# A two-layer hypergraph network: eight PSUM banks in one ring, batches written out, edge weights loaded early, and another opening

## The reference

```
H  = (adj != 0);  w = adj[first row]
Dn = 1 / (H @ w);  Be = 1 / H.sum(axis=1)
conv(x, W, b) = Dn * (H @ (Be * (H^T @ (x @ W^T)))) + b
h0 = relu(layernorm(x))
h  = layernorm(relu(conv(h0, W1, b1))) * gamma + beta
out = x + h0 + conv(h, W2, b2)
```

## Time and profile before

| | |
|---|---|
| three runs | 691.07, 691.65, 693.44 us |
| median | 691.65 us |
| profiled execution, span from first to last instruction | 692.0 us |
| TensorE busy | 636.5 us (92%), 4744 matmuls |
| VectorE busy | 510.2 us (74%) |
| ScalarE busy | 294.0 us (42%) |
| GpSimd busy | 83.6 us (12%) |
| mean granted clock of TensorE | 0.973 of full |

### The profile page before, as it was taken

How to read it: one execution, slowest core, us unless ns; L and a number is a source line. 1 busy time by engine, 2 the same in 40 slices (tenths; PEclk the granted TensorE clock), 3 DMA queues, 4 the chain that set the end, 5 groups by cost and what they waited for, 6 DMA issues and landing times.

```text
span 692.0 us, 12544 instructions
## 1 busy us (share of the span) xinstructions
PE 636.5 (92%) x4744; PEld 468.2 (68%) x4744; DVE 510.2 (74%) x1224; ACT 294.0 (42%) x538; POOL 83.6 (12%) x48
## 2 busy tenths in 40 slices
PE   4675999999989989999998998999999899999997
PEld 3432575778756776668756686586885578676886
DVE  6999877996479954799467984689747996558732
ACT  4144384354252642535415362254624364223720
POOL 2426002001120020200202002020022002000000
PEclk9888899999998999999999999999999999999999
DMA  8984960009940099302990059800796009500701
GB/s 318 230 326 92 333 123 1 1 1 197 262 182 1 1 222 291 129 1 31 235 346 29 1 103 201 337 1 1 151 238 251 1 1 229 107 1 0 183 2 62
DMA packets 146221, 90.38 MB, mean 131 GB/s; under 512 B 134768, under 2 KB 135408, under 8 KB 141168
## 3 DMA queue, kind: packets, MB, share of 16 engines
q1 hardware_dynamic: 146160, 89.54, 49.5%
HBM read 47.58 MB, written 8.39 MB: 81 GB/s over the span
## 4 chain that ended last, share of the span: by engine, by line
DVE 33%; PE 32%; SPq 11%; DMA 8%; issue 7%; ACT 7%; DVEq 0%; ACTq 0%
PE narrow L463 9%; SPq L241 8%; PE narrow L475 7%; PE wide L432 7%; DVE incidence L719 6%; DVE junk L728 5%; PE wide L416 4%; DMA edge_weights<-adj 4%; DMA z<-z_split_ring 3%; PE narrow L451 3%; DVE stat L704 3%; DVE z L785 2%; SPq L248 2%; DVE stat L789 2%; DVE h_split L710 2%
## 5 line engine op out<-in xcount | busy, mean ns | idle before, releaser
L463 PE MATMUL narrow<-xw_split,incidence 128*128 128x256 f16 x1024 | 118.4, 279 | 9.5 <-DVE edge_means L824 9.5
L463 PEld LDWEIGHTS narrow<-xw_split,incidence 128*128 128x128 bf16 x1024 | 101.9, 100 | 26.1 <-DVE edge_means L824 10.8
L416 PE MATMUL wide<-incidence_t,edge_means 128*128 128x512 bf16 x512 | 115.1, 386 | 3.9 <-DVE edge_means L862 3.9
L475 PE MATMUL narrow<-edge_means,incidence_t 128*128 128x256 f16 x1024 | 114.1, 273 | 1.5 <-DVE residual L843 1.5
L475 PEld LDWEIGHTS narrow<-edge_means,incidence_t 128*128 128x128 bf16 x1024 | 99.7, 98 | 16.1 <-DVE residual L843 3.1
L397 PE MATMUL narrow<-h_split,incidence 128*128 128x257 f16 x448 | 99.0, 273 | 4.7 <-DVE edge_means L862 4.6
L511 ACT ACTIVATE edge_means<-narrow,edge_inverse 128x256 f16<-128x256 f32 x124 | 57.4, 475 | 105.0 <-PE narrow L463 64.7
L728 DVE SCALAR_TENSOR_TENSOR junk<-incidence,edge_weights 128x1024 f32<-128x1024 bf16 x64 | 77.7, 1215 | 28.9 <-DMA edge_weights<-adj 28.9
L399 PE MATMUL narrow<-h_split,incidence 128*128 128x256 f16 x448 | 98.9, 273 | 0.0
L416 PEld LDWEIGHTS wide<-incidence_t,edge_means 128*128 128x128 f16 x512 | 50.6, 99 | 65.4 <-DVE edge_means L862 5.3
L451 PE MATMUL narrow<-w_split,z 128*128 128x256 f16 x768 | 87.7, 276 | 7.7 <-issue 6.7
(11 more groups left out here) (89 smaller groups left out, 640.2 us busy)
## 6 DMA issues: line engine op xcount, KB each, us to landing
adj_in<-adj SPq DMA_DIRECT2D x32, 1024.0 KB, 11.7
out<-residual SPq DMA_DIRECT2D x32, 256.0 KB, 2.8
x_in<-x SPq DMA_DIRECT2D x7, 1024.0 KB, 6.6
edge_weights<-adj SPq DMA_DIRECT2D x8, 512.0 KB, 4.9
x_in<-x SPq DMA_DIRECT2D x2, 512.0 KB, 4.6
z<-w2t SPq DMA_DIRECT2D x1, 512.0 KB, 5.6
z<-w1t SPq DMA_DIRECT2D x1, 512.0 KB, 8.3
incidence_t<-incidence SPq DMA_TRANSPOSE x32, 5.4
```

The lines of the kernel that those rows point to most:

```text
L416: last = nc.tensor.matmul(wide[j][:, :], edge[:, et, part, P * dt:P * (dt + 1)], inc_t[:, b.slot, 4 * half:4 * (half + 1), et, :], start=( ...
L463: last = nc.tensor.matmul(acc[:, 0:DOUT], inc[:, b.slot, ct, P * et:P * (et + 1)], xw[:, ct, part, :], start=(ct == 0 and part == HI), sto ...
L475: last = nc.tensor.matmul(acc[:, 0:DOUT], inc_t[:, b.slot, ct, et, :], edge[:, et, part, :], start=(et == 0 and part == HI), stop=(et == T ...
```

## The change

- PSUM becomes one tensor `acc` of eight banks, and `place` gives each tile of each stage its bank, in the order in which the stages run. Each stage waits for the drain of the tile that had the bank eight tiles before. Counts of edges are read four at a time.
- The loops of all engines are written out.
- `step` loads the edge weights first, before the stores, not behind the transposes of H.
- GpSimd adds h0 and b2 in eight pieces each instead of four and one; in batches 0 and 1 it adds b2 first and h0 after.
- Opening: b2 and adj come right after x; W1 is loaded behind two transposes of H, beta, gamma and W2 later still. The x statistics of batch 0 are made in two halves. Degrees 0 to 3 come before the edge means, 4 to 7 behind. The factor of W1 is found and applied alone before B's drains of batch 0; W2 is multiplied with beta and gamma, its largest found and W2 scaled only when z of batch 0 has its statistics. Incidence and h0 of batch 1 are made between the drains of C of batch 0, the z statistics behind them. x and adj of batch 2 are loaded behind the turned z of batch 0.

```diff
+        acc_ring = ctx.enter_context(nc.psum_tensor("acc", [P, RING, BANK], F32))
+            if stage == "A":
+                at = (0, 3 * T)[k] if opening else 8 * T + 4 + PER_BATCH * (k - 2)
+            elif stage == "B":
+                at = T if first else 5 * T + PER_BATCH * (k - 1)
+            elif stage == "C":
+                at = T + 4 if first else 6 * T + 4 + PER_BATCH * (k - 1)
+            elif stage == "D":
+                at = 4 * T + PER_BATCH * k - (T if last else 0)
+            elif stage == "E":
+                at = 5 * T + 4 + PER_BATCH * k - (T + 4 if last else 0)
+            else:
+                at = 7 * T + 4 + PER_BATCH * k - (2 * T + 4 if last else 0)
+            return (at + i) % RING
...
             def step(b, load=True, turn_h=True, turn_z=True):
+                if turn_h:
+                    load_edge_weights(b.next(2))
                 for q in range(QUARTERS):
...
                     for q in range(QUARTERS):
                         transpose_inc(b.next(2), q)
-                    load_edge_weights(b.next(2))
...
+                for t in range(T):
+                    pool.wait_ge(u_ready, b.count(T, t + 1))
+                    nc.gpsimd.tensor_tensor(x_in[:, t, :], x_in[:, t, :], u[:, t // GT % 2, t % GT, :],
+                                            ALU.add).then_inc(x_added, 1)
...
             def stage_a(b):
-                        acc = take_narrow(b, et, t1_ready, out_ready, b.next(-2))
+                    pe.wait_ge(out_ready, b.next(-2).count(T, et + 1))
...
             def stage_b(b):
-                        pe.wait_ge(c_drained, b.count(T, 5 + j - T))
+                        pe.wait_ge(xf_ready, b.next(-1).count(T, j + 1))
...
             def stage_c(b):
-                    if t >= 4:
-                        pe.wait_ge(c_drained, b.count(T, t - 3))
+                    if not (isinstance(b.loop, int) and b.offset == 0):
+                        pe.wait_ge(t2_ready, b.next(-1).count(T, t + 1))
...
             def stage_d(b):
-                        acc = take_narrow(b, t, xf_ready, t1_ready, b.next(1))
+                        pe.wait_ge(t1_ready, b.next(1).count(T, t + 1))
...
             def stage_e(b):
-                    acc = take_narrow(b, et, t2_ready, xf_ready, b)
+                    elif et < 4:
+                        pe.wait_ge(xf_ready, b.count(T, et + 5))
+                    else:
+                        pe.wait_ge(pt_ready, b.next(1).count(4, et - 3))
...
             def stage_f(b):
-                    acc = take_narrow(b, ct, out_ready, t2_ready, b)
+                        pe.wait_ge(c_drained, b.next(1).count(T, ct + 1))
...
-            with pe.Fori(0, N - 2, 2) as n:
-                for k in range(2):
...
+            for n in range(N - 2):
+                stage_d(Batch(0, n))
+                stage_b(Batch(0, n + 1))
```

ScalarE's opening:

```diff
+            act.wait_ge(w1_scale, 5)
             copy(w1s[:, :, HI, :], w1f, scale=wr[:, 2:3])
             copy(w1f, w1f, scale=wr[:, 2:3]).then_inc(w_hi, 1)
+            drain_b(b0, 0)
...
+            z_split(b0, 0)
+            z_split(b0, 1)
+            act.wait_ge(w2_scale, 5)
             copy(w2s[:, :, HI, :], gf, scale=wr[:, 3:4])
             copy(gf, gf, scale=wr[:, 3:4]).then_inc(w_hi, 1)
             for t in range(T):
+                if t >= 2:
+                    z_split(b0, t)
+                t1_hi_part(b1_, t)
```

VectorE's opening:

```diff
+            for ct in range(4):
+                degree(b0, ct)
+            for half in range(2):
+                edge_inverse(b0, half)
+                for et in range(T // 2 * half, T // 2 * (half + 1)):
+                    t1_lo_part(b0, et)
+            dve.wait_ge(w1_loaded, 16)
+            largest(0, w1f).then_inc(max_here, 1)
+            degree(b0, 4)
+            degree(b0, 5)
+            factor(0, w1_scale, 1.0 / (H0_SCALE * PT_SCALE * W_SCALE))
+            b_lo(b0, 0)
+            b_lo(b0, 1)
+            degree(b0, 6)
+            degree(b0, 7)
...
+            inverse_root(z_ln, z_step, b0, Z_STEPS, ZN_SCALE)
             dve.wait_ge(gamma_w2, 1)
+            largest(1, gf).then_inc(bias_step, 1)
...
+            z_lo(b0, 0)
+            z_lo(b0, 1)
+            factor(1, w2_scale, 1.0 / (ZN_SCALE * W_SCALE * XW_SCALE))
```

493 lines of the change are left out of this document (300 added, 193 removed).

## The result

| | before | after |
|---|---|---|
| median, us | 692.55 (691.07 to 693.69, 4 runs) | 662.48 (661.79 to 663.38, 4 runs) |
| ratio | | 0.9555, 95% interval 0.9528 to 0.9582 |
| span of the profiled execution, us | 692.0 | 661.6 |
| opening: stage B of batch 1 starts at | 106.55 | 107.50 |
| from there to the end of the span | 585.45 | 554.10 |

The forecast was 666.0 us, so the sign, the size and in the main the mechanism were right, and 3.5 us were left over. The table already says where the gain is: all of it behind 107.50, and the rebuilt opening is 0.95 us longer than the old one.

A forecast was written before the change was run, and what follows sets the result against it. TensorE was taken to bound the kernel behind 106.55 us, VectorE in the opening. Opening 111.2 + rest 554.6 + 0.5 for small waits gave 666.3 us of span, 0.35 over the median: 666.0 us, range 655 to 678.

The forecast's parts named there:

- Parts 1 to 3: Behind the opening: early edge weights, eight banks and written-out loops together return 30.4 of 30.9 us lost.
- the ring: Eight PSUM banks in one ring: drain waits of stages A and F and slow matmuls behind them go, 6 to 8 us.
- the jumps: TensorE's two jumps back in its loop: writing it out removes both gaps and the slow D, 8.4 us.
- Part 4: Rebuilt opening: z may be split from 83.7, but stage B of batch 1 starts at 111.2, 4.7 us later than before.
- the second all-reduce: Opening, GpSimd's maximum for W2: largest at 85.0, all-reduce ends at 89.7, dependent factor steps at 90.8.
- only its shown 0.37, 106.9: Bound for the opening: if the W2 all-reduce costs only its shown 0.37 us, B of batch 1 starts at 106.9.
- GpSimd's lock: Opening: GpSimd's adds stop VectorE; smaller pieces lose 14 us instead of 18, a gain of 4.
- The first: Rival: opening gains too, GpSimd's pieces fall between VectorE's, B of batch 1 starts near 100, total 655 us; chance 0.18.
- The second: Rival: written-out code stalls at the same places from code fetch, the 8.4 us stay, 674 us; chance 0.08.
- the fourth: Rival: TensorE waits a little at many tiles, 678 us, or 757 with some stages at 1.2 GHz; chance 0.05.
- The third: Rival: opening loses to GpSimd tiles between 13 dependent statistics steps or slow D pairs, 673 to 675 us; chance 0.15.
- The fifth: Rival: GpSimd's sixteen pieces a batch delay VectorE, bound beyond 0.7 us a piece, 723 us at 1.2; chance 0.04.

The follow-up runs named there:

- both2: Changed kernel with b2 additions moved later, W2 scaled before the z split, and bias, node factor and first edge inverse ahead of two low z parts: 654.59 us.
- pool_whole: Changed kernel with GpSimd's adds from batch 2 on in the old large pieces, four and one of 2048 columns: 661.97 us.
- early: Kernel before with only the edge weights loaded early, at the head of SyncE's step: 675.00 us.
- both: Changed kernel with the b2 additions moved to stage E of batch 0 and W2 scaled before the z split: 656.77 us.
- w2_early: Changed kernel with W2, gamma and beta loaded earlier and W2 scaled before the z split: 662.36 us.
- base_whole: Changed kernel with GpSimd's first b2 addition in batches 0 and 1 as one operation of 2048 columns: 667.01 us.

## Why the prediction was right, and where it was off

The sum had 111.2 us of opening and 555.1 behind it, 666.3 of span. Measured were 107.50 and 554.10: 3.7 and 1.0 less. Between span and median lay 0.9 us instead of the -0.35 I took. That makes 3.5.

The -0.35 had the wrong sign. The profiled execution of after took 663.38 us, 1.8 more than its own span, and in the twelve other kernels the difference is 1.7 to 2.1. The 692.0 of before was the span of one execution, set beside the median of others. With 1.8 the forecast would have been 668; that the printed one is nearer is luck.

**Parts 1 to 3 in sum: right.** Of the 30.9 us lost behind the opening I gave back 30.4; 31.35 came back. Reading the plain length of each stage off the trace of before and adding them up gave the floor to half a microsecond, 554.6 against 554.10, and eight kernels reached it within 0.3. The 0.5 us for small new waits wasn't needed. A slip inside the 30.9: 0.5 of A's 4.6 us of waits lies ahead of 106.55, so F and D had 1.8 and not 1.3.

**The shares of the parts: right in the total, too simple one by one.** They aren't terms of a sum. With the old banks the early weights are worth 18.8 us in the loop and 25.1 (583.32 to 558.26) with it written out; in the ring 13.1. Writing out is worth 2.1, 8.35 or 7.3. The ring, with the smaller edits that no run separates from it, is worth 4.2 when the other two are there, and 16.1 (583.32 to 567.23) when the weights are late. My 8.4 for the jumps was right only in company; my 6 to 8 for the ring was too high, since F's waits and a part of A's went with the late weights. Also the new load isn't issued "early in stage E" but at E's end, behind the last degree:

```profile
134.15 0.33 SPq L272 DMA_DIRECT2D edge_weights<-adj  x1
```

E runs to 135.28 there. A load lands 3.7 us later (median), and the one of the next batch, issued at 211.64, is first used at 256.38: the cover is 40 us, far more than the 14 I named.

**Part 4: direction right, 3.7 us too dear.** Step by step from the same points:

| | forecast | measured |
|---|---|---|
| z split starts | 83.7 | 82.25 |
| second factor ready | 90.8 | 86.6 |
| W2's two copies done | 92.9 | 88.8 |
| z split done on ScalarE | 104.4 | 100.7 |
| B of batch 1 starts | 111.2 | 107.50 |

The mis-sized term is the second all-reduce. In the kernel before it stood 4.7 us between input and result, and I took that as its own cost. VectorE and ScalarE of after:

```profile
83.48 0.16 DVE L1086 SCALAR_TENSOR_TENSOR weight_max<-weight_max 128x1 f32<-128x1 f32 x1
...
85.21 0.69 DVE L913 TENSOR_TENSOR z_split_ring<-z,z_split_ring 128x512 f16<-128x512 f32 x1 [0.70 <-ACT z L632]
85.82 0.15 DVE L1001 TENSOR_SCALAR weight_max_all<-weight_max_all 128x1 f32<-128x1 f32 x1
...
82.25 0.81 ACT L631 ACTIVATE z_split_ring<-z,z_ln 128x512 f16<-128x512 f32 x1
...
86.62 1.15 ACT L592 ACTIVATE w_split<-xw_split,weight_factor 128x1024 f16<-128x1024 f32 x1 [1.45 <-DVE weight_factor L1009]
```

The input is complete at 83.64, the result is there at 84.16: 0.5 us, and the factor then waits only for VectorE's own low part of z, to 85.82. The 4.7 us was a delay that runs from the end of GpSimd's operation before; there that was 28.04, 1.2 us ahead of the input, and here GpSimd had been idle for 13.08 us. The page of before had said so: "5.59 <-issue" in the earlier trace rows is idle time with nothing to wait for, and I read past the word. I had the other end of the bound, "only its shown 0.37, 106.9", 0.6 us from what was measured, which is in part luck (below); the value was taken from the nearest row, which stood under another condition.

Not all of the 3.7 us is this term. 1.45 of it is there before, with the z split's start. The all-reduce was 4.2 us too dear, but since the factor then waited for VectorE, the stretch from z split to factor is only 2.75 shorter than forecast (4.35 instead of 7.1); the six tiles behind it took some 0.5 longer. So 106.9 came close by errors that cancelled. And the sign "GpSimd's second all-reduce in the chain that ended last" didn't come: the chain runs through VectorE's second low part to the factor.

The same mechanism on the other side I missed: an ordinary operation behind an all-reduce starts 7 to 9 us late. It costs C 2.5 and D 4.1 us of waiting; D's first tiles start at 93.71 where its z was turned sooner. It is worth 1.4 us at most, since A and C of the opening have room.

**Smaller terms.** GpSimd's lock: the sixteen incidence rows of the opening take 14.2 us instead of 24.1, the eight low parts 6.9 instead of 7.8, and single steps lose some 7.5 (4.4 in those of 128x4; of those of 128x8 the largest is 2.10 us instead of 0.17, at 48.76, beside the subtraction for W1); about 13 lost where I took 14. The term was right, and gives 1 of the 1.45 us by which the z split came early; A of batch 0 took 3.3 us more than its plain length (17.33 instead of 14.03, last section). "As many microseconds in total" was wrong: the tiles take 0.85 us each in the steady part and not 0.6. A of batch 0 ended at 34.44 (forecast 31), C at 61.26 (58), A of batch 1 began at 73.30 (74), and the hole before it was there, from the end of C to 73.30.

**The rivals.** The first (opening near 100) didn't come about, but its room was real: both2 takes it, at 99.36. The second (gaps in straight code) and the fourth (small waits at many tiles) are excluded by 0.11 us of idle time in 550.96. With the fourth falls the reading that goes with it: by the Trainium skill ("TensorE: Matmul & The Clock Gate", A second HAM failure mode: psum-queue depth-cycling) a kernel that cycles through banks can swing between both clock levels; here the clock stayed at 1.00 through some 300 tiles of such cycling, so the trace gives no instance of it. The third had its mechanism right, dependent steps each behind a tile, and its price too high: five steps of 0.65 and a few others, not thirteen for each set. The fifth was nearer than its 0.04 allowed by my own rule: a piece takes 0.85 us and the rule had VectorE the bound from 0.7 on. Yet nothing was lost, and pool_whole shows the pieces cost nothing: the rule charged each piece in full to VectorE, whose busy time behind the opening instead is 401.81 us with the small pieces in after and 407.22 with the large ones in pool_whole.

## What to carry to other kernels

Add up the undisturbed lengths of the bound engine's stages from the trace of before: that floor forecast this result better than any account of the single waits, because such waits share causes and an edit that removes one alone may only move it (2.1 us alone, 8.35 with the other). More buffers take in late drains, not late data: first find the load that the engine in the middle waits for. And where a row gives the cost of an operation, look whether its idle time says "issue" before taking the distance from input to result as the operation's own.

## What was not expected of the hardware

GpSimd loses time when it changes between an all-reduce and an ordinary addition, unless the time is hidden by a longer wait for the input. The all-reduce starts 5.5 to 6.4 us after the end of the ordinary operation before it though its input is there (5.59, 5.53 in early, 6.11 and 5.99 in the rows above, 6.35 in both), and 0.1 to 0.3 us after its input when GpSimd has been idle for 13 us or more. The way back takes 8.67 and 7.20 us in after, 7.42 and 6.73 in w2_early and both2 for W2, and 6.7 to 8.7 in every kernel with the new opening and an all-reduce, but for W1 in both and both2: there it takes 10.77 and 11.70, and C waits 4.6 and 5.5 us for it. What makes these two longer is open. By the Trainium skill ("GPSIMD Engine Reference", Instruction dispatch) the first call of a freshly loaded routine pays about 6 us that no instruction in the profile shows. The trace agrees in size for the way there, with 5.5 to 6.4; it also shows it again at the second all-reduce and, longer, on the way back. That a routine is loaded then, no run here shows.

TensorE's first matmuls after 17.11 us of idle start 0.21 us apart, at the pace of the 1.2 GHz level, and from 23.06 on 0.11 apart, while the granted clock reads 1.00 in both stretches; rows of after:

```profile
22.42 0.42 PE L422 MATMUL acc<-h_split,incidence 128*128 128x256 f16 x1
22.63 0.42 PE L420 MATMUL acc<-h_split,incidence 128*128 128x257 f16 x1
22.85 0.40 PE L422 MATMUL acc<-h_split,incidence 128*128 128x256 f16 x1
23.06 0.30 PE L420 MATMUL acc<-h_split,incidence 128*128 128x257 f16 x1
```

28 of these matmuls cost 3 us, the most of what A of batch 0 takes over its plain 14.03. In pool_whole, whose A starts at 17.28 and whose opening is the same, it is 14 of them, so the number differs from run to run with no edit to explain it (15 in base_whole). So in an opening the spacing of matmuls says more of the clock than the granted one does. The kernel before had no slow start. There the product of beta and W2, which the change moved behind C, stood just ahead of A:

```profile
9.45 3.78 PE L483 MATMUL narrow<-z 128*128 128x256 f32 x8 [9.45 <-DVE z L885]
13.94 0.27 PE L379 MATMUL wide<-h_split,incidence 128*128 128x257 f16 x1 [0.71 <-DVE h_split L710]
14.05 0.27 PE L381 MATMUL wide<-h_split,incidence 128*128 128x256 f16 x1
```

A's matmuls are 0.11 apart from the first. So the change may have paid up to 3 us for moving that product; filling the idle in the new opening was not tried.
